# A head's operands written in place from a doubled projection, its transfers left out, and the loads, statistics and table load of the prologue reordered

## The reference

```
x = x + layernorm(attn(layernorm(x)))      # 16 heads of 64, causal, and a graph network on the attention
x = x + layernorm(ffn(layernorm(x)))       # 2 layers of local attention and a gated feed-forward
```

```
q = (xn @ Wq) heads * 64 ** -0.5 ; k = (xn @ Wk) heads ; v = (xn @ Wv) heads
attn = softmax(causal(q @ k.T)) ; out = attn @ v
adj = clip(attn + I, 0, 1) ; deg = rowsum(adj) ; feats = v
twice: feats = gelu(adj @ (feats @ w[l] + b[l]) / deg + feats)
out = layernorm((out + feats @ lin_w + lin_b) @ Wo) * gamma_out
```

## Time and profile before

| | |
|---|---|
| median of 3 runs | 1573.04 us |
| lowest and highest | 1572.93 and 1578.7 us |
| the profiled execution | 1574.63 us |
| its span, first to last instruction | 1572.8 us |
| mean granted clock of TensorE | 0.975 |
| busy: PE, DVE, ACT, POOL | 1441.3, 1181.4, 995.3, 367.7 us |

### The profile page before, as it was taken

How to read it: one execution, slowest core, us unless ns; L and a number is a source line. 1 busy time by engine, 2 the same in 40 slices (tenths; PEclk the granted TensorE clock), 3 DMA queues, 4 the chain that set the end, 5 groups by cost and what they waited for, 6 DMA issues and landing times. The chain is left out here.

```text
span 1572.8 us, 29162 instructions
## 1 busy us (share of the span) xinstructions
PE 1441.3 (92%) x10194; PEld 1109.0 (71%) x10194; DVE 1181.4 (75%) x3237; ACT 995.3 (63%) x2307; POOL 367.7 (23%) x474
## 2 busy tenths in 40 slices
PE   4899999999999999999999999999788999999896
PEld 3577877778777787777777777777455666666663
DVE  4577777777777777777878777776787888888875
ACT  2366666666666666666666666666355877778573
POOL 2022222221122111222222222223222332222211
PEclk8899999999999999999999999999987999999998
DMA  6021111211112111121111121220300000100100
GB/s 172 14 51 32 28 28 29 43 39 28 28 31 48 32 28 28 31 44 35 28 28 28 38 45 28 58 48 1 91 21 11 21 21 21 25 18 21 28 12 20
DMA packets 41147, 54.36 MB, mean 35 GB/s; under 512 B 11774, under 2 KB 23978, under 8 KB 41002
## 3 DMA queue, kind: packets, MB, share of 16 engines
q1 hardware_dynamic: 41002, 52.51, 15.0%
HBM read 9.89 MB, written 1.05 MB: 7 GB/s over the span
## 5 line engine op out<-in xcount | busy, mean ns | idle before, releaser
L1098 ACT ACTIVATE t<-PS 128x512 f32<-128x512 f32 (+3 forms) x384 | 188.9, 492 | 148.4 <-PE PS L661 94.5
L1544 DVE TENSOR_REDUCE t<-PS 128x1 f32<-128x512 f32 (+3 forms) x384 | 210.7, 550 | 77.3 <-PE PS L634 54.4
L1561 DVE TENSOR_TENSOR t<-t 128x512 fp32r<-128x512 f32 (+3 forms) x384 | 211.5, 551 | 9.6 <-ACT t L1099 9.4
L1099 ACT ACTIVATE t<-PS 128x512 fp32r<-128x512 f32 (+3 forms) x384 | 188.6, 491 | 0.0
L713 PE MATMUL PS<-t 128*128 128x512 f32 (+3 forms) x384 | 150.1, 391 | 21.9 <-ACT t L1132 21.6
L632 PE MATMUL PS<-t 128*128 128x512 f32 (+3 forms) x384 | 140.8, 391 | 24.8 <-DMA t<-t 13.0
L1248 ACT ACTIVATE t<-PS,t 128x128 f32<-128x128 f32 x256 | 113.2, 463 | 67.7 <-DVE t L1804 67.7
L660 PE MATMUL PS<-t 128*128 128x512 f32 (+3 forms) x384 | 149.0, 388 | 2.7 <-DMA t<-t 2.2
L1408 POOL TENSOR_TENSOR t<-t 128x16 f32<-128x16 f32 x32 | 92.8, 2900 | 234.1 <-DVE t L1666 234.1
L678 PE MATMUL PS<-t 128*66 128x512 f32 (+3 forms) x384 | 138.8, 361 | 0.0
L661 PE MATMUL PS<-t 65*128 65x512 f32 (+3 forms) x384 | 133.7, 348 | 0.0
(11 more groups left out here) (189 smaller groups left out, 3872.5 us busy)
## 6 DMA issues: line engine op xcount, KB each, us to landing
t<-t SPq DMA_DIRECT2D x188, 128.0 KB, 2.3
t<-t SPq DMA_DIRECT2D x64, 256.0 KB, 3.4
t<-in_c_rot SPq DMA_DIRECT2D x4, 512.0 KB, 5.6
t<-in_L_ffn_wqkv SPq DMA_DIRECT2D x2, 768.0 KB, 7.6
t<-in_L_attn_Wv SPq DMA_DIRECT2D x2, 512.0 KB, 7.4
out<-t SPq DMA_DIRECT2D x4, 256.0 KB, 2.3
t<-in_L_ffn_w SPq DMA_DIRECT2D x2, 341.0 KB
t<-in_L_attn_x SPq DMA_DIRECT2D x2, 256.0 KB, 3.2
```

Source lines behind the costliest of these rows:

```text
L1098: e.activation(Es[:, k % NS, 0:n], b[:, 0:n], ACT.Exp).then_inc(a_es.up((t, k)), 1)
L1099: e.activation(Eh[:, o:o + n], b[:, 0:n], ACT.Exp).then_inc(a_eh.up((t, k)), 1)
L1544: e.tensor_reduce(n[:, c, ib:ib + 1], bank(k % 2)[:, 0:hi - lo], AX.X, ALU.max, negate=True).then_inc(d_max.up((t, k)), 1)
L1561: e.tensor_tensor(El[:, o:o + n], Es[:, k % NS, 0:n], f32(Eh[:, o:o + n]), ALU.subtract).then_inc(d_el.up((t, k)), 1)
```

## The change

For head 0 alone, the projection is made with two weights instead of one: `twins` holds for K and for Q the head's 64 columns twice side by side, high and low part (`twins` lies in the first 512 columns of `El`, which is written only once scores are there). So both halves of the partitions get K in one bank and Q in another. ScalarE writes K high to `K1`, Q high to `Q1` and its lower half to `Q2`, and VectorE K low to `K2` and Q low to the upper half of `Q1`. `part(0)` and `double(0)` are gone, and `smax` and `scores` of head 0 wait for the engines. Besides:

- gamma_in is the second load; the two `gb` loads follow the masks; then come `part(1)` and `double(1)`; then the nine loads for `WG`, `WW1`, `WO`, `linw`, `linb` and x's second batch; then `mrow(0)`. `wqkv0`, `bandF`, `shm` and `gam_out` are issued in turn 4 of the loop.
- VectorE does both statistics before the first scaling.
- ScalarE does an Exp on 16 columns first.
- GpSimd widens Wk and Wq for head 0 into `twins`, and the V weights (`widen_v`) of heads 0 and 1 behind `widen(1)`.
- TensorE and the others take the order given at the end of the diff; `proj(1, c)` waits for head 0's reads of banks 4 and 5, and `values` uses banks 6 and 7.

```diff
@@ sync
+            e.dma_start(gam_in[:], I["L0_attn_gamma_in"].rearrange("(d a) -> d a", a=1)).then_inc(ld["gin"], 16)
             e.dma_start(x0[:, 4:8, :], x_tiles[:, 4:8, :]).then_inc(ld["xb"], 16)
...
-            part(0)
-            double(0)
-            for t in range(NH):
+            part(1)
+            double(1)
+            q.wait_ge(*d_zero["WG"])
...
+            e.dma_start(x0[:, 8:16, :], x_tiles[:, 8:16, :]).then_inc(ld["xc"], 16)
+            mrow(0)
+            for t in range(1, NH):
                 if t + 1 < NH:
                     part(t + 1)
                 mrow(t)
                 if t + 1 < NH:
                     double(t + 1)
+                if t == 4:
+                    e.dma_start(wqkv0, I["L0_ffn_wqkv"][0]).then_inc(ld["wqkv0"], 16)
...
@@ tensor
+            def head0(c):
+                q.wait_ge(*d_turn[c])
+                q.wait_ge(*w_wd[0])
+                sl = slice(c * 512, (c + 1) * 512)
+                for i in range(2):
+                    b = bank(2 + 2 * i + c)
+                    e.matmul(b, twins[:, i, 0, :], xh[:, sl], start=True, stop=False)
+                    e.matmul(b, twins[:, i, 1, :], xh[:, sl], start=False, stop=False)
+                    m = e.matmul(b, twins[:, i, 0, :], xl[:, sl], start=False, stop=True)
+                m.then_inc(p_proj.up((0, c)), 1)
...
                 if t == 1:
-                    q.wait_ge(*a_val["T", c])
-                elif t:
+                    q.wait_ge(*a_q0[c])
+                    q.wait_ge(*d_low[0, c])
+                else:
                     q.wait_ge(*a_eh[t - 2, 10 + c])
...
+            def operands(t):
+                if t:
+                    q.wait_ge(*twice(t))
+                else:
+                    q.wait_ge(*d_low[0, 1])
+                    q.wait_ge(*a_q0[1])
...
             turn(0, 0)
             turn(1, 1)
-            values()
-            for c in range(2):
-                proj(0, c, 2 + c)
-            for c in range(2):
-                proj(1, c, 4 + c)
-            for c in range(2):
-                projv(0, c)
-            for k in range(NTL):
+            head0(0)
+            head0(1)
+            values(0)
+            values(1)
+            proj(1, 0, 4)
+            proj(1, 1, 5)
+            smax(0, 0)
+            smax(0, 1)
+            mixed(0)
+            mixed(1)
+            smax(0, 2)
+            smax(0, 3)
+            projv(0, 0)
+            projv(0, 1)
+            for k in range(4, NTL):
                 smax(0, k)
@@ scalar
+            def head0(c):
+                sl = slice(c * 512, (c + 1) * 512)
+                q.wait_ge(*p_proj[0, c])
+                q.wait_ge(*d_zero["ini"])
+                e.copy(K1[0][:, sl], bank(2 + c)).then_inc(a_k0.up(c), 1)
+                e.activation(Q1[0][:, sl], bank(4 + c), ACT.Copy, scale=0.125)
+                e.activation(Q2[0][0:64, sl], bank(4 + c)[0:64, :], ACT.Copy, scale=0.125).then_inc(a_q0.up(c), 1)
...
+            q.wait_ge(*w_half[0])
+            e.activation(fsc[:, 0:1], half[:, 0:1], ACT.Exp)
             turn(0)
             turn(1)
...
+            head0(0)
+            head0(1)
+            values(0)
+            values(1)
+            proj(1, 0, 4)
+            proj(1, 1, 5)
+            mixed(0)
+            mixed(1)
+            projv(0, 0)
+            projv(0, 1)
             mrow(0)
@@ gpsimd, widen(t)
+                if t == 0:
+                    for i, (W, name) in enumerate(((WkD, "wk"), (WqD, "wq"))):
+                        q.wait_ge(ld[name], 16)
+                        src = W[:, 0:1, :].broadcast_to([P, 2, DH])
+                        hi, lo = [twins[:, i, s, :].rearrange("p (a d) -> p a d", a=2) for s in range(2)]
+                        e.tensor_copy(hi, src).then_inc(own.up(), 1)
+                        q.wait_ge(*own.now())
+                        m = e.tensor_tensor(lo, src, hi.bitcast(F32), ALU.subtract)
+                    m.then_inc(w_wd.up(t), 1)
+                    return
...
             widen(0)
             widen(1)
+            widen_v(0)
+            widen_v(1)
             widen(2)
+            widen_v(2)
@@ vector
+            def head0(c):
+                sl = slice(c * 512, (c + 1) * 512)
+                q.wait_ge(*a_k0[c])
+                e.tensor_tensor(K2[0][0:64, sl], bank(2 + c)[0:64, :], f32(K1[0][0:64, sl]), ALU.subtract)
+                q.wait_ge(*a_q0[c])
+                e.scalar_tensor_tensor(Q1[0][64:P, sl], bank(4 + c)[64:P, :], 0.125, f32(Q1[0][64:P, sl]), ALU.mult,
+                                       ALU.subtract).then_inc(d_low.up((0, c)), 1)
...
-            normed(0, 4)
-            normed(4, 4)
+            q.wait_ge(*ld_x[0])
+            ln_stats(("in", 0), x0, 0, 4, True)
+            q.wait_ge(*ld_x[1])
+            ln_stats(("in", 4), x0, 4, 8, True)
+            ln_apply(("in", 0), xn, x0, 0, 4)
+            ln_apply(("in", 4), xn, x0, 4, 8)
             turn(0, 0)
             turn(1, 1)
+            head0(0)
+            head0(1)
...
             for c in range(2):
-                lower(0, c, 2 + c)
-            for c in range(2):
                 lower(1, c, 4 + c)
+            for k in range(4):
+                smax(0, k)
             for c in range(2):
                 projv(0, c)
-            for k in range(NTL):
+            for k in range(4, NTL):
                 smax(0, k)
```

More of the change, by code:

```diff
@@ L274, in program @@
         a_lin = signal("a_lin", range(1, 5))
-        a_hi = signal("a_hi", halves)
+        a_hi = signal("a_hi", halves[2:])
+        a_k0 = signal("a_k0", range(2))
+        a_q0 = signal("a_q0", range(2))
         a_v = signal("a_v", halves)
@@ L486, in weights @@
                         e.dma_start(b1[l][0:n, 3 * f + c:3 * f + c + 1], src).then_inc(w, 16)
[L488 to L490 removed]
+            part(1)
+            double(1)
+            q.wait_ge(*d_zero["WG"])
+            e.dma_start(WG[:, 0:DH], I["c_ident"][0:66, 0:DH]).then_inc(ld["wg"], 16)
+            e.dma_start(WG[0:DH, DH:P], I["L0_attn_gnn_w"][0]).then_inc(ld["wg"], 16)
+            e.dma_start(WG[:, P:130], I["c_ident"][0:66, 64:66]).then_inc(ld["wg"], 16)
+            for t in range(2):
+                e.dma_start(WW1[t * DH:(t + 1) * DH, :], I["L0_attn_gnn_w"][1]).then_inc(ld["ww1"], 16)
+            e.dma_start(WO[0:DH, :, :], I["L0_attn_Wo"].rearrange("(h e) n -> e h n", h=HA)).then_inc(ld["wo"], 16)
+            e.dma_start(linw[:], I["L0_attn_lin_w"]).then_inc(ld["lw"], 16)
+            e.dma_start(linb[:], I["L0_attn_lin_b"].rearrange("(d a) -> d a", a=1)).then_inc(ld["lb"], 16)
+            e.dma_start(x0[:, 8:16, :], x_tiles[:, 8:16, :]).then_inc(ld["xc"], 16)
+            mrow(0)
+            for t in range(1, NH):
                 if t + 1 < NH:
@@ L545, in turn, with values, mixed @@
                 m.then_inc(p_turn.up(g), 1)
-            def values():
+            def values(g):
                 q.wait_ge(ld["wv"], 16)
[L549 to L552, removed]
+                for r in range(4):
+                    m = e.transpose(bank(6 + g)[:, r * P:(r + 1) * P], Wv[:, (4 * g + r) * P:(4 * g + r + 1) * P], identF[:])
+                m.then_inc(p_val.up(("T", g)), 1)
+            def mixed(g):
                 q.wait_ge(*a_val["T", 1])
                 q.wait_ge(ld["w0"], 32)
[L555 to L559, removed]
+                for r in range(4):
+                    m = e.matmul(bank(6 + g)[:, r * P:(r + 1) * P], WvT[:, (4 * g + r) * P:(4 * g + r + 1) * P], w0d[:],
+                                 start=True, stop=True)
+                m.then_inc(p_val.up(("W", g)), 1)
+            def head0(c):
[8 more added lines that the diff above has]
+                m.then_inc(p_proj.up((0, c)), 1)
             def linear(g, b):
@@ L1047, in turn, with values, mixed @@
                 e.activation(xh[:, g * 512:(g + 1) * 512], bank(b), ACT.Copy, scale=gam_in[:, 0:1]).then_inc(a_turn.up(g), 1)
[L1049 to L1055, removed]
+            def head0(c):
[5 more added lines that the diff above has]
+                e.activation(Q2[0][0:64, sl], bank(4 + c)[0:64, :], ACT.Copy, scale=0.125).then_inc(a_q0.up(c), 1)
+            def values(g):
+                q.wait_ge(*p_val["T", g])
+                e.copy(WvT[:, g * 512:(g + 1) * 512], bank(6 + g)).then_inc(a_val.up(("T", g)), 1)
+            def mixed(g):
+                q.wait_ge(*p_val["W", g])
+                e.copy(WV2[:, 8 * g:8 * g + 8, DH:P], bank(6 + g).rearrange("p (h d) -> p h d", h=8)).then_inc(a_val.up(("W", g)), 1)
             def linear(g, b):
@@ L1358, in widen, with widen_v @@
                 m.then_inc(w_wd.up(t), 1)
+            def widen_v(t):
+                if t >= NH:
+                    return
+                h, R = t % HA, WR[t % 2]
                 q.wait_ge(ld["wv2"], 16)
```

38 lines of the change are left out of this document (10 added, 28 removed).

## The result

| | kernel before | changed kernel |
|---|---|---|
| median | 1577.09 us (20 runs, 1566.92 to 1582.0) | 1568.85 us (20 runs, 1559.66 to 1576.01) |
| ratio | | 0.9949, 95% interval 0.9931 to 0.9967 |
| profiled execution, span | 1574.63, 1572.8 us | 1565.80, 1564.0 us |
| first scores matmul | 47.65 us | 37.80 us |
| row transfers of heads 0, 1, 31 | 45.73, 83.87, 1066.79 | 35.89, 79.61, 1064.97 |

The changed kernel is 8.2 us faster by the medians, 5.2 to 10.9 by the interval. I had forecast 10.1, to a time of 1562.9; the time lies 0.45 us above my range.

A forecast was written before the change was run, and what follows sets the result against it. TensorE's 9.1 us wait on a transfer ahead of head 0's maxima was taken to delay the first scores. Prologue steps summed to scores at 37.6 instead of 47.65, 10.1 us off the 1573.04 median: 1562.9, range 1558.8 to 1568.4.

The forecast's parts named there:

- parts 1 to 4: Prologue steps: statistics and gamma, head 0's weights, projection written in place, then mixing, V and maxima; scores at 37.6 us.
- SyncE: Transfer queue: nine loads behind head 1's pieces issue until 31 to 35 us, just ahead of the row wanted at 35.3.
- Two transfer stages, with the 9.1 us wait, are gone: End of the in-place projection step: head 0's operands ready at 20.4 us without transfers.
- Whatever moves it moves all that stands behind: First scores' start carries everything later with it, unless the loop's first turn finds something late; 10.1 us taken off the time.
- the last of my signs of being wrong: Prediction is wrong if first scores start ten us earlier and the second head's row does not.
- (a): Rival: TensorE's slow pace lasts through mixing, V matmuls, projection and maxima; gain 4.8 us, time 1568.2; chance 0.14.
- (b): Rival: fast level stays through maxima and first scores, the latter saving at most 3.4 us; gain 15.2, time 1557.8; chance 0.10.
- The base: Median of the kernel before, 1573.04 us (1572.93 to 1578.7), from which the 10.1 us gain was subtracted.
- Rule against row: TensorE's clock in the prologue: the skill says transposes don't count as busy; the trace agrees so far as it goes.
- one of the two moments: Fast level reached either just before 16.8 us or only after head 1's projection.
- (c): Rival: head 0's row lands behind the queued loads, scores at 41.5 us; gain 6.1, time 1566.9; chance 0.08.
- (d): Rival: SyncE blocks on issuing the nine loads, scores at 68 us; 20 us later, time 1593; chance 0.02.

The follow-up runs named there:

- no_twins: Changed kernel with head 0 sent through the two transfer stages again, new load order and front kept; profiled only, scores at 37.74 us.
- after_timed: The changed kernel unedited, timed again beside the versions with unread matmuls: median 1566.93 us over 8 runs, ratio to before 0.9928.
- late_filled: v_late plus one unread matmul before each maximum from k = 4 and on either side of the row's matmul: 1551.30 us, ratio to before 0.9837.
- v_late: Changed kernel with head 0's V matmuls behind its maxima and the row's transfer ahead of late loads; profiled only, scores 35.92 us, turn 49.8.

## Why the prediction was right or wrong

- **Prologue, parts 1 to 4 and SyncE.** Right as a sum: 37.80 against 37.6. Head 0's projection began at 12.11, not 11.4 (Wk had landed 0.7 later), ScalarE's three copies took 1.5 us instead of 2.1 (0.48 a step, last half ready at 19.2), V matmuls ran 24.21 to 27.57, the eight maxima 29.16 to 34.76, 5.6 us as taken. The pace rose at 16.05.
- **The reason given for the gain.** "Two transfer stages, with the 9.1 us wait, are gone" names only one of two ways. The wait was long because of the loads ahead and because head 0's projection stood behind the mixing; with the loads deferred and the new order kept, the transfers hide behind the V chain, and taking them away brings nothing more (`no_twins` 37.74). The sum ended on the right chain, but I did not ask what each part would do without the other.
- **The step that failed.** It is the last one, from the start of scores to the time: "Whatever moves it moves all that stands behind", taken off one median of three runs. It puts two terms at nothing without a reason. One is the difference between the kernels in head 0's turn and behind it. The turn takes 38.1 and 43.8 us in two profiles of before and 38.1 to 46.9 in three of the changed kernel, by when the level comes back, so a profile's turn was one draw; in the profiled pair it took back 5.6 of the 9.84 us, and the last of my signs of being wrong came true: the first scores start ten us earlier and the second head's row only 4.3. My rivals had the slow level ahead of the scores (a) and its absence (b), but not its length behind them. The other term is the uncertainty of the base.
- **The base.** I took 10.1 from a median of three runs, 1573.04; over 20 runs it is 1577.09, and they spread over 15 us. Two thirds of the miss of 5.95 us is here: 4.05 from the base, 1.9 from the gain (8.2 in place of 10.1, inside the interval of 5.2 to 10.9). A range drawn from the gain's steps alone was too narrow by the base's own uncertainty. The 1.9 us alone could be chance, or the loop behind head 0's turn (985.2 us on the mean of three profiles against 983.3 on two), or head 0's turn itself; no run tells which.
- **Rule against row.** "TensorE: Matmul & The Clock Gate" of the Trainium skill, on transposes: the pace rose at 16.05, after 3.9 us of head 0's matmuls (from 12.11) and before the Wv transposes, one of the two moments that I had derived by it; this doesn't test the rule. Its section "Part 1: The HAM clock gate" describes the fast level as what a busy TensorE gets and the slow one as what an idle one falls to. The fall at 26.2 fits this badly, with 2.0 us of unbroken work ahead of it and a wait of only 0.87 us ahead of that. The stay does not fit it at all: 10.00 busy us of 10.00 at 0.50 in `after_timed`. There the measurement decides.
- **Rivals.** (a) didn't happen ahead of 26 us. (b) happened in `late_filled` only, by added work: against `v_late` its scores come 2.7 us earlier and its turn is 13.2 us shorter, far above my 3.4. (c) didn't: the queue was free at 32.0, and scores followed the row's issue by 1.9 us. (d) didn't: nine issues took 25.64 to 31.99. The chance of 0.74 for faster by over 0.5% stands beside a measured 0.51%: on the bound, neither shown nor refuted.

## What to carry to other kernels

When a wait goes by several means, try each alone: here direct writing or deferred loads, each with the new order of work, brought 8 to 9 of 10 us, and the chain behind them set the end; the order alone was never tried. Before a gain of some us is read off two profiles, compare where TensorE's level changes in both, and take base and change from the same set of runs. Where a prologue leaves TensorE waiting in short pieces, unread matmuls in the gaps and dense work moved into the longest wait are worth a try: together they were worth 15.6 us here, more than the change itself.

## What the hardware showed that I had not expected

- The granted clock fell from 1.00 to 0.50 while TensorE was busy: at 26.2 us in the changed kernel, 2.0 us behind a wait of 0.87 us, and at 21.0 in `no_twins`, 1.0 us behind one of 1.63. In the ten profiles with the fp32 pairs and no added matmuls it stayed there for 17 to 44 us of mostly busy time.
- It then came back 7, 9 to 10, or 19 to 28 us behind the first scores, and head 0's turn took 37.6 to 49.8 us with it. Ten unread matmuls of 0.24 us each (the step at the fast level) were put in the gaps, with V moved into the row's hop; the level didn't fall in the profile, and the spread of the runs went from 14.5 us (eight runs) to 3.2 (five).
